# Splitting the second layer's row maxima on GpSimd instead of VectorE

## The reference

```python
def _msa(x, w_qkv, w_proj):                      # second layer's attention
    attn = jnp.einsum('bhnd,bhmd->bhnm', q, k) * (1.0 / np.sqrt(DK))
    attn = jax.nn.softmax(attn, axis=-1)         # needs each row's maximum
    y = jnp.einsum('bhnm,bhmd->bhnd', attn, v)
    return y @ w_proj
def _moe_mlp(x, gate_w, gate_b, w1, w2):
    one_hot = jax.nn.one_hot(jnp.argmax(xf @ gate_w + gate_b, axis=-1), E)
    h = gelu(einsum('td,edh->teh', xf, w1)); y = einsum('teh,ehd->ted', h, w2)
x = _layernorm(x + attention(x))                 # first layer
h = x + _msa(_layernorm(x), ...)                 # second layer
out = _layernorm(x + h + _moe_mlp(_layernorm(h), ...))
```

## Time and profile before

| | before |
|---|---|
| median of 3 runs | 1576.76 us (1574.66 to 1577.91) |
| profiled execution | 1580.19 us, its span 1578.3 us |
| PE busy | 1365.4 us, 87% |
| DVE busy | 820.5 us, 52% |
| ACT busy | 959.3 us, 61% |
| POOL busy | 330.8 us, 21% |
| mean granted clock of PE | 0.947 |

### The profile page before, as it was taken

How to read it: one execution, slowest core, us unless ns; L and a number is a source line. 1 busy time by engine, 2 the same in 40 slices (tenths; PEclk the granted TensorE clock), 3 DMA queues, 4 the chain that set the end, 5 groups by cost and what they waited for, 6 DMA issues and landing times. The chain is left out here.

```text
span 1578.3 us, 21210 instructions
## 1 busy us (share of the span) xinstructions
PE 1365.4 (87%) x6614; PEld 637.5 (40%) x6615; DVE 820.5 (52%) x1950; ACT 959.3 (61%) x1809; POOL 330.8 (21%) x337
## 2 busy tenths in 40 slices
PE   3499899898997889899999999999973799999993
PEld 1233333333333333343434343333322466666662
DVE  4233463553543267777777777777832333333331
ACT  0277776776776656666666666666641366666662
POOL 5122231332222111021212222221221111111110
PEclk9699999999999999999999999999985899999997
DMA  6211312313313212122212122121336111111113
GB/s 162 93 49 66 127 44 95 110 39 117 100 41 127 94 41 94 41 81 56 81 55 81 57 79 74 61 94 42 148 121 240 57 50 47 48 48 48 49 50 126
DMA packets 109605, 127.60 MB, mean 81 GB/s; under 512 B 8304, under 2 KB 102128, under 8 KB 109392
## 3 DMA queue, kind: packets, MB, share of 16 engines
q1 hardware_dynamic: 77696, 79.46, 15.9%
q10 hardware_dynamic: 27392, 33.56, 6.3%
q0 software_dynamic: 4432, 13.52, 2.7%
HBM read 51.51 MB, written 28.46 MB: 51 GB/s over the span
## 5 line engine op out<-in xcount | busy, mean ns | idle before, releaser
L686 ACT ACTIVATE w_space<-bank 128x512 f32<-128x512 f32 x1024 | 569.4, 600 | 300.9 <-PE bank L449 291.9
L449 PE MATMUL bank<-w_space 96*128 96x512 bf16 (+1 forms) x1024 | 366.5, 388 | 35.6 <-ACT w_space L686 21.4
L873 DVE TENSOR_REDUCE negm<-bank 128x1 f32<-128x512 f32 x512 | 327.5, 683 | 103.1 <-PE bank L476 100.2
L463 PE MATMUL bank<-w_space 128*32 128x512 f32 x2048 | 280.9, 621 | 11.4 <-ACT w_space L686 8.3
L476 PE MATMUL bank<-w_space 96*128 96x512 bf16 x512 | 199.2, 389 | 28.3 <-ACT neg_T L699 11.3
L449 PEld LDWEIGHTS bank<-w_space 96*128 96x128 bf16 (+1 forms) x1024 | 98.6, 100 | 231.1 <-ACT w_space L686 123.0
L649 PE MATMUL bank<-w_space,work_space 128*128 x624 | 142.3, 381 | 1.6 <-DVE work_space L1153 1.6
L628 PE MATMUL bank<-w_space,work_space 128*128 x312 | 142.0, 598 | 0.6 <-DVE work_space L1144 0.6
L476 PEld LDWEIGHTS bank<-w_space 96*128 96x128 bf16 x512 | 49.7, 97 | 215.0 <-DVE negm L873 104.2
L514 PE MATMUL bank<-work_space,wqkv_sb 128*128 128x512 f32 x256 | 123.3, 604 | 5.6 <-DVE w_space L993 4.8
L649 PEld LDWEIGHTS bank<-w_space,work_space 128*128 128x128 f32 x624 | 115.4, 190 | 16.6 <-issue 2.3
(11 more groups left out here) (134 smaller groups left out, 1606.2 us busy)
## 6 DMA issues: line engine op xcount, KB each, us to landing
w_space<-work_space SPq DMA_DIRECT2D x384, 128.0 KB
w_space<-in_w_dram ACTq DMA_DIRECT2D x16, 1024.0 KB, 8.4
work_space<-in_x_dram ACTq DMA_DIRECT2D x16, 512.0 KB, 4.5
work_space<-rows_dram SPq DMA_DIRECT2D x39, 128.5 KB, 2.1
work_space<-rows_dram SPq DMA_DIRECT2D x39, 128.0 KB, 2.1
x_dram<-xo SPq DMA_DIRECT2D x32, 128.0 KB, 1.7
h_dram<-row_sb SPq DMA_DIRECT2D x32, 128.0 KB, 3.3
work_space<-h_dram ACTq DMA_DIRECT2D x8, 512.0 KB, 3.8
```

The source lines that it names most:

```text
L449: nc.tensor.matmul(L.st_banks[c % n][:, :], k_stack[0:L.rows, s, h, kt * P:(kt + 1) * P], q_stack[0:L.rows, s, h, :], start=True, stop=Tru ...
L463: last = nc.tensor.matmul(L.pv_banks[g % n][VW * j:VW * (j + 1), :], v_aug[:, s, kt, HEADS_AT_ONCE * g + j, :], probs[:, q % 2, j, :], sta ...
L686: nc.scalar.activation(probs[:, q % 2, j, :], L.st_banks[c % len(L.st_banks)][:, :], ACT.Exp, scale=SCALE).then_inc(L.exps, 1)
L873: ve.tensor_reduce(negm[:, c % TT, c // TT:c // TT + 1], L.mx_ring.bank(use)[:, :], axis=AX.X, op=ALU.max, negate=True).then_inc(L.mx_ring ...
```

## The change

`neg_split` goes from DVE's queue to POOL's. It stands there at the start of the same quads, in front of that quad's tasks and behind all tasks of earlier quads. `negm` gets two buffers, chosen by g % 2, and the first reduction of a group waits until the split two groups before has been done. The arithmetic is the same.

```diff
-        negm = sb("negm", [P, TT, HEADS_AT_ONCE])
+        negm = sb("negm", [P, 2, TT, HEADS_AT_ONCE])
...
             def max_tile(L, b, g, c, s):
                 use = ("MX", g, c)
                 dve.wait_ge(*L.mx_ring.full(b, use))
-                ve.tensor_reduce(negm[:, c % TT, c // TT:c // TT + 1], L.mx_ring.bank(use)[:, :],
+                before = GROUPS * (b - L.first) + g - 1
+                if c == 0 and before > 0:
+                    dve.wait_ge(L.neg_ready, before)
+                ve.tensor_reduce(negm[:, g % 2, c % TT, c // TT:c // TT + 1], L.mx_ring.bank(use)[:, :],
...
                 for q in range(QUADS):
                     mx = max_tiles(q, par, projected, attended)
-                    for L, b, g, s in neg_group(q, par, projected, attended):
-                        neg_split(L, b, g)
...
+            def neg_split(L, b, g):
+
+                last_tile = HEADS_AT_ONCE * TT - 1
+                pool.wait_ge(*L.mx_ring.empty(b, ("MX", g, last_tile - 1)))
+                pool.wait_ge(*L.mx_ring.empty(b, ("MX", g, last_tile)))
+                if g:
+                    pool.wait_ge(*L.mx_ring.full(b, ("NG", g - 1)))
+                elif not isinstance(b, int) or b > L.first:
+                    pool.wait_ge(*L.mx_ring.full(b - 1, ("NG", GROUPS - 1)))
+                n = 3 * GROUPS * (b - L.first)
+                pool.tensor_copy(neg_parts[:, :, 0, :], negm[:, g % 2, :, :]).then_inc(L.neg_step, 1)
+                pool.wait_ge(L.neg_step, n + (3 * g + 1))
...
+                pool.tensor_tensor(neg_parts[:, :, 2, :], neg_rest[:, :, :], neg_parts[:, :, 1, :],
+                                 ALU.subtract).then_inc(L.neg_ready, 1)
...
-                for slot in SLOTS:
-                    outer_tasks(slot, par, projected, finished, task)
+                for q in range(QUADS):
+                    for L, b, g, s in neg_group(q, par, projected, attended):
+                        neg_split(L, b, g)
+                    for j in (0, 2):
+                        outer_tasks((q, j), par, projected, finished, task)
```

More of the change, by code:

```diff
@@ L1216, in _ @@
             pool.wait_ge(consts_in, 16 * N_FIRST)
+            def neg_split(L, b, g):
[9 more added lines that the diff above has]
+                pool.wait_ge(L.neg_step, n + (3 * g + 1))
+                pool.tensor_tensor(neg_rest[:, :, :], negm[:, g % 2, :, :], neg_parts[:, :, 0, :],
+                                 ALU.subtract).then_inc(L.neg_step, 1)
+                pool.wait_ge(L.neg_step, n + (3 * g + 2))
+                pool.tensor_copy(neg_parts[:, :, 1, :], neg_rest[:, :, :]).then_inc(L.neg_step, 1)
+                pool.wait_ge(L.neg_step, n + (3 * g + 3))
+                pool.tensor_tensor(neg_parts[:, :, 2, :], neg_rest[:, :, :], neg_parts[:, :, 1, :],
+                                 ALU.subtract).then_inc(L.neg_ready, 1)
             def task(L, name, b, s):
```

## The result

The change makes the kernel slower. The changed kernel takes 1613.42 us (median of 4 runs, 1604.91 to 1619.42), the kernel before 1575.71 us beside it (4 runs, 1574.11 to 1577.91); the ratio is 1.0234, with a 95% interval of 1.0186 to 1.0283. The profiled execution has a span of 1611.5 us, against 1578.3.

A forecast was written before the change was run, and what follows sets the result against it. PE was taken to bound the kernel, with the split on its path. POOL's pace 12.0, queue 20.4 and clock 10 us sum to 42.4 on the profiled 1580.2, giving 1622.6, or 1619 as a median; range 1598 to 1642.

The forecast's parts named there:

- What bounds the kernel: Second-layer stages: PE sets the time, working 70.4 of 74.68 us; the split is already on PE's path in most groups.
- what is taken away: DVE's queue loses 32 splits of 0.79 us, 25 us; PE's wait remains, and the second buffer alone buys nothing.
- POOL's pace: At the splits, leaving out the queue: each group 0.4 us later on POOL, group 3 0.85; together 12.0 us.
- the lower bound: At each split: with 0.19 us for a POOL operation, a group is 0.3 us later.
- twice VectorE's time: Splits at the skill's rule: 0.35 us an operation, a group about 0.9 us later, the sum some 14 us larger; 1633.
- The queue: Quad 2 of six stages: group 1's split waits on POOL behind the scatter's landing; 20.4 us in all.
- 6 to 8 us longer: Sign in the profile: stages that begin behind a scatter lengthen by 6 to 8 us.
- 1 to 2 us: Sign in the profile: stages that do not begin behind a scatter lengthen by 1 to 2 us.
- The clock: Behind the six long PE waits: a 3.4 us stretch at half clock each, 1.7 us apiece, taken as 10 us.
- What is given back: PE's small waits during stalls: nothing taken back; the rival had half vanish in six stages, 13 us, 9%.
- The sum: Whole kernel: 12.0 + 20.4 + 10 = 42.4 us on the profiled 1580.2 gives 1622.6; as a median 1619.
- the rival in which the clock holds: No clock loss behind the long waits, the other terms as forecast: 1609 us, 12%.

The follow-up runs named there:

- group 1 alone: The changed kernel with only group 1's split on POOL and groups 0, 2 and 3 on DVE, against the kernel before: 1611.16 us, ratio 1.0215.
- the other set: The changed kernel timed once more beside the kernel before, to stand beside a kernel with added filling matmuls: 1621.66 us, ratio 1.0279.
- the tiles first: The changed kernel, landing wait still in front, with the next group's first two tiles before the transposes on PE's queue, against the kernel before: 1596.7 us, ratio 1.0106.

## Why the prediction was right

**What bounds the kernel; what is taken away.** Right. DVE lost 25.4 us of work (25 forecast) and the time didn't fall; the second buffer alone measures as nothing (1.0007, 0.998 to 1.0035).

**POOL's pace.** The mechanism was right and the term too large. A split takes 4 operations of 0.20, 0.22, 0.20 and 0.22 us with 0.08 between them (0.22 each forecast), and 1.06 us in all (1.12 forecast). PE starts 0.05 us behind POOL's end (742.45 to 742.50), and not 0.15 as in the earlier trace rows. So a group is 0.3 us later, which was the lower bound, instead of 0.4. In front of the transposes PE idles more by 2.4 us for group 0 (3.2 forecast), 2.1 for group 2 (2.8) and 3.9 for group 3 (6.0). For group 3 the growth per wait is 0.56 us (0.56 before, 1.12 now) and not 0.85. Half of that difference is the same 0.15 us; the other half is that the split does not begin 0.08 us behind the norm's end, as the forecast has it, but 0.06 in front of it (785.42, with the norm's end at 785.48):

```profile
784.84 0.64 POOL L1273 TENSOR_TENSOR row_sb<-row_sb,rows_sb 128x256 f32<-128x256 f32 x1
785.42 0.20 POOL L1209 CAST neg_parts<-negm 128x16 bf16<-128x16 f32 x1
...
786.54 0.39 PE L487 MATMUL bank<-ident_bf,neg_parts 128*12 128x128 bf16 x4 [1.12 <-POOL neg_parts L1216]
```

Together 8.3 us instead of 12.0.

By twice VectorE's time, as the Trainium skill has it for operations with two inputs (GPSIMD Engine Reference, section 4.1), an operation would have been 0.35 us by estimate; the two subtractions took 0.223 against VectorE's 0.174, a ratio of 1.3. So the rule did not hold for 16 elements. The prediction put all four operations at twice (by its own terms 15 us more in the sum, not 14); two of them are conversions with one input, which took 0.197 against 0.174.

**The queue.** Right in mechanism and place, and nearly in size: the six waits behind a scatter grew PE's idling in front of group 1's transposes from 0.6 to 19.1 us, 18.5 more, where 20.4 were forecast. The landing took the time that it took before, as the forecast needs: from start to end the six scatters sum to 62.1 us in both profiles. The landing wait moved behind the split takes them away, group 1 alone brings them back, and the order of PE's queue leaves them as they are. The sign "6 to 8 us longer" was met by three of the five stages (7.4, 8.2 and 6.5 us); the other two are 3.9 and 6.1 us longer, of which the first kept its clock. "1 to 2 us" for a stage without the stall is met by the kernel with the landing wait moved: 75.92 us, 1.2 more than before.

**The clock.** Right in sign, and the 10 us were a little low. In the changed kernel's profile five of the six long waits have a stretch at the lower level at their end or just behind it. The one of 2.75 us, in the stage shown at 1.00 above, is not, so I was wrong that each one is. Two of the five stretches were twice as long, and a further one fell elsewhere. Just behind the longest wait:

```profile
743.00:746.40 3.40, 3.22 (x8) 1.51 (x8) 2.07 (x3) 1.50 (x3) 0.00 (x0) 0.51 0.03 8
```

One such stretch costs a stage 1.45 us (77.37 against 75.92), against the 1.7 that I took from half a clock. In all, PE's busy time grew by 13.9 us while its time at the lower clock rose from 10.2 to 41.0 us. One stretch of 3.4 us in that rise is not the change's: the kernel before has one just in front of its first transposes (at 559.24), the changed one just behind them. That leaves some 12 us, an estimate from 13.9 us of work for 30.7 us at the lower clock. In both kernels there are six of the first-layer waits that the forecast leaned on, not seven as the earlier trace rows says: a lower stretch goes with all six before, and with five of six in the changed kernel. That the runs of the changed kernel spread over 1604.9 to 1619.4 us fits stretches that fall now one way and now another; it was not tested.

**What is given back.** I took nothing; by the difference between PE's idling in front of the transposes (+26.8) and in all (+23.7) it was 3 us.

**The sum.** 26.8 us of waiting where 32.4 were forecast, 13.9 us of slower matmuls where 10 were, less 3: 37.7 us, against 42.4. The waiting came out 5.6 us too high: about half from the crossing (0.1 us in each of 29 groups), 1.7 from the operations (0.06 in each), 1.0 from where group 3's split begins. The clock, 3.9 too low, and the 3 given back, taken as nothing, nearly cancel. The forecast of 1619 us is 5.6 us too high, 4.7 by this sum and 1.1 by the kernel before, whose median is 1575.7 in this set and not 1576.8.

That the medians moved by the same 37.7 us (1613.42 less 1575.71) is in part luck: the two profiled spans differ by 33.2, and the other set has the changed kernel 2.8% above the kernel before instead of 2.3. Nor does the time by itself decide for the forecast. 1613.4 lies at the lower edge of its 1612 to 1629, nearer to the 1609 of the rival in which the clock holds than to 1619, and the runs reach from 1605 to 1619. The waits, the clock and the experiments decide.

## What to carry to other kernels

An engine's busy share says nothing of what a moved instruction will wait for: read, at the very place where it will stand, what is queued in front of it and whether that waits. An idle engine that waits for a DMA to land is as closed as a busy one, and moving that wait behind the urgent work gave back four fifths of the loss here. Giving work to another engine paid here only when the first one had something to do meanwhile. It needed the next group's tiles in front of the wait, and even then only the three groups whose split does not stand behind POOL's norm were worth moving, as far as the runs tell: 0.9895 with those three on POOL (0.9868 to 0.9923), against 0.994 with none (0.9919 to 0.9961) and 0.9931 with all four.

## What the runs showed of the hardware

POOL's operations on 16 elements are nearer to DVE's than I had expected: 0.197 us for a conversion and 0.223 for a subtraction, against 0.174 and 0.174 on DVE. From POOL to PE the crossing took 0.05 us at the splits and 0.15 at L557. The clock does not make the difference, since L557 has 0.15 at full clock too (POOL's end 1157.82, PE's start 1157.97 in the kernel before); what does wasn't tried.

PE's clock fell at long waits, but not at each, and at some short ones. Four profiles have the landing wait in front of group 1's split: the changed kernel twice, group 1 alone on POOL, and the tiles first. They have 24 waits of 2.3 to 5.1 us there. At 22 of them a stretch of 3.4 or 6.8 us at the lower clock began, between 2.8 us before the wait's end and 2.2 us behind it; the two exceptions are waits of 2.30 and 2.75 us. Seven profiles have 49 waits of 1.1 to 1.2 us in front of group 3's transposes, and behind ten of them such a stretch began, 1.7 to 2.3 us after the wait. So the length of one wait does not tell whether the clock falls.
